# Subtractions in quarters, six split parts in place of four, and another order and unread products around the first experts

## What is computed

```python
    logits = xn @ router_weight.T + router_bias
    probs = jax.nn.softmax(logits, axis=-1)
    _, idx = jax.lax.top_k(logits.T, top_k)          # 16 experts x 256 tokens
    xe = xn[idx]
    h = jnp.einsum('ecd,efd->ecf', xe, fc1_weight) + fc1_bias[:, None, :]
    h = jax.nn.gelu(h, approximate=False)
    y = jnp.einsum('ecf,edf->ecd', h, fc2_weight) + fc2_bias[:, None, :]
    gates = jnp.take_along_axis(probs.T, idx, axis=1)
    output = zeros.at[idx.reshape(-1)].add((y * gates[:, :, None]).reshape(-1, d))
    gate_sums = zeros1.at[idx.reshape(-1)].add(gates.reshape(-1, 1))
    output = jnp.where(gate_sums > 0, output / gate_sums, output)
```

## Time and profile before

| | before |
|---|---|
| median of 3 runs (lowest to highest) | 1163.67 us (1163.33 to 1165.07) |
| the profiled execution, and its span | 1165.49 us, 1163.7 us |
| busy: TensorE, its weight loads | 1022.4 us (88%), 647.5 us (56%) |
| busy: VectorE, ScalarE, GpSimd | 821.7 (71%), 671.3 (58%), 786.4 us (68%) |
| mean granted TensorE clock | 0.942 of full |
| chain that ended last | TensorE 72%, VectorE 14%, GpSimd 4%, ScalarE 3% |

### The profile page before, as it was taken

The page is one execution under the profiler, slowest core; times in us unless marked ns, Lnnn a source line. Parts: engine busy times, 40 slices in busy tenths (PEclk is TensorE's granted clock), DMA queues, the critical chain, the costliest instruction groups (busy, mean ns, idle before and its releaser), DMA issues.

```text
span 1163.7 us, 17671 instructions
## 1 busy us (share of the span) xinstructions
PE 1022.4 (88%) x6090; PEld 647.5 (56%) x6090; DVE 821.7 (71%) x1899; ACT 671.3 (58%) x1301; POOL 786.4 (68%) x880
## 2 busy tenths in 40 slices
PE   3679999999999999999998998999740399999996
PEld 2545445545645645554564564544320378999995
DVE  6876867876786786787769667775268765667752
ACT  6646676575577567657657665534424135566662
POOL 3116895896698689679669966967703157777773
PEclk9859999999999999999999999989965598999998
DMA  6020020010002002001200000000127137666652
GB/s 180 1 59 1 1 59 1 1 55 25 20 1 80 22 5 73 23 0 38 63 19 1 2 26 19 2 22 1 38 60 216 46 75 206 196 214 216 217 166 27
DMA packets 73881, 72.02 MB, mean 62 GB/s; under 512 B 39008, under 2 KB 67808, under 8 KB 69696
## 3 DMA queue, kind: packets, MB, share of 16 engines
q1 hardware_dynamic: 66672, 62.12, 16.9%
q0 software_dynamic: 6336, 8.70, 4.2%
q10 hardware_dynamic: 784, 0.07, 0.1%
HBM read 56.98 MB, written 13.83 MB: 61 GB/s over the span
## 4 chain that ended last, share of the span: by engine, by line
PE 72%; DVE 14%; POOL 4%; ACT 3%; issue 3%; DMA 2%; SPq 1%; DVEq 0%; ACTq 0%; POOLq 0%
PE bank L812 54%; PE pair_bank L812 12%; POOL prob_sum L1368 2%; ACT probs L1106 2%; PE bank L845 2%; DVE c_in L1756 2%; PE bank L893 2%; DVE maxima L1649 1%; DVE masked_scores L1656 1%; DVE root_y L1467 1%; DMA c_in<-in_ctx 1%; DVE root_t L1466 1%; DVE qk_nat L1625 1%; DVE in_stats L1472 1%; DVE root_t L1465 1%
## 5 line engine op out<-in xcount | busy, mean ns | idle before, releaser
L1368 POOL TENSOR_TENSOR prob_sum<-prob_sum,probs 128x256 f32<-128x256 f32 x628 | 464.7, 771 | 78.3 <-ACT probs L1106 71.4
L1106 ACT ACTIVATE probs<-bank,mask_col 128x512 f32<-128x512 f32 x256 | 161.9, 684 | 117.2 <-PE bank L812 109.8
L1656 DVE CUSTOM_DVE_ANT_0 masked_scores<-pair_bank,mask_bias 128x512 bf16<-128x512 f32 x256 | 166.2, 687 | 84.9 <-PE pair_bank L812 84.4
L812 PE MATMUL bank<-probs,v_nat 128*64 128x512 f32 x768 | 206.6, 626 | 0.2 <-ACT probs L1106 0.2
L1649 DVE TENSOR_REDUCE maxima<-pair_bank 128x2 f32<-128x1024 f32 x64 | 78.3, 1223 | 50.4 <-PE pair_bank L812 50.4
L1106 ACT ACTIVATE probs<-bank 128x512 f32<-128x512 f32 x128 | 69.3, 593 | 66.7 <-PE bank L812 66.6
L812 PE MATMUL bank<-q_hi,k_hi 64*128 64x512 f32 x384 | 91.7, 470 | 17.5 <-ACT probs L1106 16.1
L812 PE MATMUL pair_bank<-k_hi,q_hi 64*128 64x512 f32 x384 | 94.0, 485 | 13.4 <-DVE maxima L1656 8.7
L812 PEld LDWEIGHTS bank<-q_hi,k_hi 64*128 64x128 f32 x384 | 37.4, 185 | 103.1 <-ACT probs L1106 54.7
L1346 POOL TENSOR_TENSOR z_lo<-z_full,z_hi 128x512 fp32r<-128x512 f32 x32 | 40.9, 1284 | 63.3 <-ACT z_hi L1106 63.3
L812 PEld LDWEIGHTS pair_bank<-k_hi,q_hi 64*128 64x128 f32 x384 | 37.4, 190 | 80.3 <-issue 44.1
(11 more groups left out here) (244 smaller groups left out, 2546.3 us busy)
## 6 DMA issues: line engine op xcount, KB each, us to landing
w_raw<-in_fc SPq DMA_DIRECT2D x16, 1024.0 KB, 4.8
w<-in_fc SPq DMA_DIRECT2D x16, 1024.0 KB, 5.4
c_in<-in_ctx SPq DMA_DIRECT2D x16, 384.0 KB, 3.4
x_in<-in_x SPq DMA_DIRECT2D x8, 512.0 KB, 5.1
out_x<-x_in SPq DMA_DIRECT2D x8, 512.0 KB, 3.8
rows_scratch<-xr_nat SPq DMA_DIRECT2D x8, 512.0 KB, 3.0
c_in<-in_ctx SPq DMA_DIRECT2D x16, 128.0 KB, 3.4
b_rows<-in_fc_bias SPq DMA_DIRECT2D x16, 128.0 KB, 5.5
```

What stands on the lines that cost most here:

```text
L812: return pe.matmul(out, lhsT, rhs, start=start, stop=stop, skip_group_check=True)
L1106: return act.activation(out, a, f, bias=bias, scale=scale)
L1368: last = tt(total[:, half], first[:, half], p[:, half], ALU.add)
L1656: last = dve.tensor_tensor_reduce(masked_scores[:, hh, :], pair_bank[:, hh, :], mask_bias[:, 512 * g:512 * (g + 1)], 1.0, MASKED, ALU.add, ...
```

## The change

Four edits:

1. FS goes from 4 to 6: six of the eight parts of the second product are made of three products of rounded operands; `h_hi`, `h_lo`, `w2_hi`, `w2_lo` grow from four parts to six.
2. GpSimd makes every half of `w1_lo` in four instructions of 256 columns, in place of one of 1024 (two of 512 for experts 0 and 1). The semaphore rises after the fourth.
3. Around expert 1: `renew_rows` goes from the end of expert 0 to after the first part of expert 1, which for SyncE is behind the load of expert 2's second weight; `split(2, 1)` goes from after part 9 and the scatters to after part 3 and ahead of them; the second part of the list of group 3 goes from after part 17 to after part 21, behind the turning of expert 2's tokens.
4. `warm`: products of 512 columns whose result nobody reads, on TensorE: 8 after `order(0)`, 1 after the first list is counted, 9 after it is spread, 4 in `order(1)` behind the totals, 5 after the tokens of expert 0 are turned.

```diff
-SPLIT_FROM, FS = 2, 4
+SPLIT_FROM, FS = 2, 6
...
         add("order", 1)
         add("turn_tokens", 0)
+        add("warm", 5)
         add("slots", 1)
...
                     add("gather", 2)
                     add("gather_gates", 2)
-                    add("renew_rows")
...
     add("order", 0)
+    add("warm", 8)
     add("slots", 0)
     for part in range(2):
         add("list_hot", 0, part)
-    for piece in ("list_count", "list_join", "list_spread"):
+    add("list_count", 0)
+    add("warm", 1)
+    for piece in ("list_join", "list_spread"):
         add(piece, 0)
+    add("warm", 9)
     add("gather", 0)
...
+            if at == 1 and e == 1:
+                add("renew_rows")
+                add("split", 2, 0)
+            if at == (3 if e == 1 else 9) and e + 1 < E:
+                add("split", e + 1, 1)
             if at == (9 if e == 1 else 4):
                 for c in range(2):
                     add("scatter", e - 1, c)
-            if at == 1 and e == 1:
-                add("split", 2, 0)
-            if at == 9 and e + 1 < E:
-                add("split", e + 1, 1)
             if at == 13 and e + 2 < E:
                 add("split", e + 2, 0)
             if at == 10 and e + 2 < E:
                 add("gather", e + 2)
-            if at in (9, 17) and lists:
-                add("list_hot", lists, at // 17)
+            if at == 9 and lists:
+                add("list_hot", lists, 0)
+            if at == (3 * FT - 3 if e == 1 else 17) and lists:
+                add("list_hot", lists, 1)
...
                     mm(list_bank[:, total_place][:, experts], all_ones[:], totals, True, True).then_inc(searched.sem, 1)
+                    if part:
+                        warm(4)
+
+        def warm(n):
+
+            on.wait_ge(*w_hi_made.at(0, 0))
+            for _ in range(n):
+                mm(bank[7], w1_hi[0][:, 0, 0:P], w1_hi[0][:, 0, 0:512], True, True)
...
-            if e >= 2:
-                tt(w1_lo[i][:, n, :], w1_raw[i][:, n, :], as32(w1_hi[i][:, n, :]),
-                   ALU.subtract).then_inc(w_lo_made.sem, 1)
-                return
-            for part in range(2):
-                at = slice(part * F // 2, (part + 1) * F // 2)
-                on.wait_ge(*trial_made.at(FIRST_SPLITS[2 * e + n] + 2 + part))
+            for part in range(4):
+                at = slice(part * F // 4, (part + 1) * F // 4)
+                if e < 2 and part % 2 == 0:
+                    on.wait_ge(*trial_made.at(FIRST_SPLITS[2 * e + n] + 2 + part // 2))
                 last = tt(w1_lo[i][:, n, at], w1_raw[i][:, n, at], as32(w1_hi[i][:, n, at]), ALU.subtract)
             last.then_inc(w_lo_made.sem, 1)
```

More of the change, by code:

```diff
@@ L1095, in tensor_program @@
         work = {"search": search, "order": order, "list_count": list_count, "list_spread": list_spread,
-                "turn_tokens": turn_tokens, "hidden": hidden, "expert_out": expert_out}
+                "turn_tokens": turn_tokens, "warm": warm, "hidden": hidden, "expert_out": expert_out}
         for kind, *at in expert_plan:
```

## The result

The changed kernel takes 1180.46 us (median of 6 runs, 1179.09 to 1182.42) against 1163.50 for the kernel before (6 runs, 1159.31 to 1165.07): a ratio of 1.0149, 95% interval 1.0134 to 1.0164. It is slower by 17 us, outside the predicted range. The profiled execution took 1180.82 us, its span is 1179.0.

The account below looks back on a forecast made before the run. TensorE bounds the experts before the change; after it GpSimd's queue was to bound odd experts with a list. Terms: -4.7 to expert 3, then +5.0 - 1.5 - 0.9 = +2.6, together -2.1 us: 1161.6 us, range 1155 to 1168.5.

Parts of the forecast that it names:

- the cover of the extra work: Loop from expert 2: ScalarE's extra 1.4 us an expert hidden at 25.5 of 40 us busy; VectorE's additions costed by length.
- 0.3 alone: Second list part in odd experts: first of VectorE's two list operations, 1.05 us with its wait on GpSimd, 0.3 without.
- the sum of the odd expert: Odd expert with a list: GpSimd's fetches, quarters, scatters and quarters end at 13.7 us, not 12.69; GpSimd's queue becomes the bound.
- The saving: Six split parts for four: 0.30 us less per expert from 2 on, 4.2 us over 14, if TensorE stays the bound.
- VectorE's wait on quarters: VectorE's operations beside GpSimd's quarter subtractions: each waits 0.7 us at most, while pushing the remaining quarters back.
- The two scatters were kept at 3.70 us: GpSimd's pair of scatters: 3.70 us, unchanged; the first takes 1.82 beside VectorE's hidden-half subtractions, the second 1.58.
- I am wrong if GpSimd's loop keeps idle time in every pair: Sign against the forecast: GpSimd still idles in every pair of experts; before the change it idled some 5.0 us of 27.13.
- Even experts: Even experts in the loop: GpSimd's quarters end at 12.5 us, before TensorE's 14.14, so each saves 0.30.
- First experts: Expert 2 starts at 958.8 us with TensorE's 4.02 us stand cut to about 1.4; expert 3 at 974.6, 4.7 earlier.
- the slower rival: Odd experts: VectorE's weight subtraction slips ahead of GpSimd's last quarter; 1.5 us more each, up to 1170.6 us; chance 0.18.
- Unread products: Choice of tokens before expert 0: the fill lifts TensorE's clock, -1.2 us; bounds -1.2 and +0.8.
- forecast -4.7 up to expert 3 and +2.6 for the loop: Expert 3 starts at 974.6 against 979.26 (-4.7); then odd experts +5.0, even -1.5, experts 13 to 15 -0.9: +2.6.

Follow-up runs that it names:

- e3: The kernel before with only six split parts in place of four; 1184.24 us, ratio 1.0183.
- e5: e3 with VectorE's multiplications of the hot columns one place earlier in odd experts; 1185.33 us, ratio 1.0195.
- e9: e3 with both multiplications of the hot columns behind xe_lo of the next expert; 1179.50 us, ratio 1.0129.
- e10: e3 with the list's two comparisons in the even expert before and the multiplications where the comparisons stood; 1168.61 us, ratio 1.0043.
- e13: e10 with scale_out of odd experts behind the next expert's third h_lo and their scatters one step later; 1173.71 us, ratio 1.0083.
- e16: e3 with GpSimd subtracting only 512 of 1024 columns of each weight half from expert 2 on, the rest not computed; 1161.30 us, ratio 0.9979.
- e7: e3 with 20 unread products of 128x256 in TensorE's stand ahead of even experts 4 to 12; 1178.44 us, ratio 1.0133.
- e8: The whole change but with four split parts kept; 1165.00 us, ratio 1.0022 to the kernel before.
- e4: The changed kernel with four split parts and whole subtractions from expert 2 on; 1163.97 us, ratio 1.0010 to the kernel before.
- e1: The whole change, but GpSimd subtracts 1024 columns at a time from expert 2 on; 1180.86 us, ratio 1.0155 to the kernel before.
- e2: The kernel before with only the quarter subtractions from expert 2 on; 1164.99 us, ratio 1.0018.

## Why the prediction was wrong

**The step that failed** is the cover of the extra work. Of ScalarE's it says "at 25.5 of 40 us busy that is hidden"; for VectorE's no cover was named at all. Its two h_lo and the longer subtraction were costed by length, 0.75 + 0.55 us, against 29.2 busy of 40. A busy share is a mean over a pair of experts; the extra work falls into every expert, and in the odd ones VectorE also builds the list. It was not the extra 1.3 us as such that cost: the same work moved GpSimd's second subtraction 2.5 us back, so that VectorE's multiplication met its beginning and not its end. The wait in it grew from 0.6 us (1.05 against 0.49 alone; I had read 0.3 alone into the earlier trace rows) to 3.3 us. e3 shows the shift, e5, e9, e10 and e13 that whatever VectorE has there takes the wait, and e16 that with the subtraction halved six parts are no slower: 2.3 us faster than the kernel before.

The same step in the sum of the odd expert: there the two list operations push back GpSimd's quarters only, and GpSimd's subtraction was to end last, at 13.7 us after TensorE's start. It ended at 12.22 (1082.11 against 1069.89), ahead of the 12.39 at which TensorE wanted it. What came last was xe_lo, over at 14.25, behind the two operations in VectorE's own queue. That path had no term.

**The saving was right.** An expert with no list to count and whose next tokens are not late takes 12.40 us, as in the forecast (12.69 - 0.30 = 12.39): experts 13 and 14 of the changed kernel, and the odd experts of e9, e10 and e16.

**VectorE's wait on quarters, "0.7 us at most", was wrong** for the one instruction that mattered. Its fp32 subtractions did slip in between quarters (w2_lo took 2.12 us, 0.4 over its 1.76 alone), but the bf16 tensor_scalar of line 1887 stood through all four, 2.6 us over its 0.49 alone. So the quarters did not help where it counted, and the odd experts' 14.33 us (forecast 13.7) have this cause, not GpSimd's queue. The sentence "I am wrong if GpSimd's loop keeps idle time in every pair" came true: 2.60 us a pair. The two scatters were kept at 3.70 us and took 4.4 in this odd expert (1074.88 to 1079.28). The 1.82 us of the first one were read as the price of VectorE's h_lo beside it; here it has six h_lo beside it and takes 1.63, so that reading was at best a part of it.

**Even experts** were to take 14.14 and took 16.29. I had no term for the clock. Behind the stand of 1.9 us ahead of them it fell to 1.2 GHz each time; e7 prices that at 1.2 us a pair. And list_join behind the fifth h_lo holds TensorE 0.6 us (0.9 in e7, where the clock stays up): the h_lo come at ScalarE's pace of 0.81 us, two activations each, where TensorE makes an h every 0.71.

**First experts: right in place, wrong in what follows.** Expert 2 starts at 957.77 (forecast 958.8), expert 3 at 975.05 (974.6). But I let the gain of 4.7 us stand. In e8, with four split parts, the same start is followed by 9.3 us lost in experts 3 and 4. The event behind it is close to the one of the slower rival, VectorE's w2_lo at the last quarter. In the changed kernel:

```profile
986.04 6.13 POOL L1420 TENSOR_TENSOR w_lo<-w_raw,w_hi 128x256 fp32r<-128x256 f32 x4
```

```profile
985.96 1.09 DVE L1887 TENSOR_SCALAR hot_ids<-hot_lo,token_in_tile 128x1024 bf16<-128x1024 bf16 x1
986.97 1.75 DVE L1888 TENSOR_TENSOR hot_ids<-hot_lo,tile_ids 128x1024 bf16<-128x1024 bf16 x1
...
989.58 2.03 DVE L1934 TENSOR_TENSOR w_lo<-w,w_hi 128x1536 fp32r<-128x1536 f32 x1 [0.26 <-ACT w_hi L1121]
```

The last quarter begins at 989.27 and takes 2.90 us beside w2_lo, and TensorE stands 3.35 for the four. I had placed that rival at five odd experts and at 0.15 us of margin; it came once, where GpSimd was behind, and as a part of the loss of 8.8, not as the loss of the loop.

**Unread products: right.** The granted clock rose (1.00 from 918 us on, 0.50 before). From VectorE's first write of `earlier`, 1.2 us ahead of the first unread product, to xe_lo of expert 0 it is 15.53 us in the kernel before (15.5 to 15.9 in the twelve profiles without unread products) and 14.1 to 15.0, 14.5 on average, in the seven with them: 1.0 us, forecast 1.2. The start of that xe_lo in the table moved by 2.9, but the rest lies ahead of the first unread product, where the profiles differ by 6 us from one to another. In the median of e4 nothing of the gain is seen: 1 us is lost again in its longer first experts.

**In sum:** forecast -4.7 up to expert 3 and +2.6 for the loop from there; measured by xe_lo -6.6 up to expert 3 (-2.9 - 3.7; 1.6 of it is only that this profile reached the choice of tokens earlier) and +22.2 from there, 8.8 in experts 3 and 4 and 13.4 behind them. The loop is what was wrong.

## What to carry to other kernels

"Hidden" needs an address: name the instruction beside which the added work lies and the one it pushes back, and ask what that one then meets on another engine. Two queues that share something (here VectorE and GpSimd) have a phase to each other, and a shift of it by 2.5 us turned 0.6 us of wait into 3.3; moving the instruction that shows the wait handed it to the next one, at a better or a worse place. A gain at the head of a pipeline is not yet a gain of the whole: follow the engine that was behind two rounds further.

## What the runs showed of the hardware

GpSimd's 128x1024 subtraction shut out VectorE until it was over (the multiplication ended 0.28 or 0.29 us behind it in the kernel before, e1, e3 and e16 alike), and of VectorE's instructions every sort with SBUF inputs alone that stood there: a bf16 tensor_scalar (3.79 us, 0.49 alone), a bf16 tensor_tensor (4.53, 1.21 alone), an fp32 tensor_scalar (3.44 for two, 0.60 alone) and fp32 subtractions (4.01 for three, some 1.2 alone). By the records each of these began 0.5 to 0.6 us ahead of the subtraction, while an indirect DMA of GpSimd was still running; what held VectorE in that first half microsecond is not shown. The Trainium skill ("SBUF — State Buffer", who interferes with whom) states this for a VectorE instruction with two SBUF inputs or in a two-port mode; the rows agree on the kinds. I had used it for one instruction and not for its neighbours.

Not expected was that four subtractions back to back are not always four chances: VectorE's fp32 subtractions slipped in between quarters, and so did a bf16 tensor_tensor (1.75 us, 1.21 alone), but the bf16 multiplication, where it came after the first quarter had begun, waited for all that were left: 3.07 us in four experts of the changed kernel, 1.44 in e2. Where it came 0.08 us ahead of the first quarter, in expert 3 of the changed kernel, it took 1.09.

Nor that the second scatter's record stretches to 3.60 us, against 1.58 with nothing beside it. VectorE's two comparisons run beside it there, but they are not shown to be the cause: in the kernel before they overlap it too and it takes 1.79, and in the changed kernel, with the comparisons at the same distance as in e3, it takes 2.46. Elsewhere in the changed kernel scatters took up to 3.14 us.

TensorE's stands of 1.9 us in the changed kernel were each followed by some 4 us with a granted clock of 0.57, but the length of the stand does not decide it alone: behind stands of 2.65 us the clock stayed at 1.00 twice of four times in e1, and in e9 twice behind stands of 1.78. Stands of 0.6 us at list_join and of 1.3 and 1.4 at list_spread (e10, e13) left the spacing at 0.118 us.
